# Attention and routed experts on one core: maxima 45 steps ahead, the router's product folded into the values', the last body's slots, scatters and pads interleaved anew

## The chip, the cores and the metric

The kernel runs on one core of a Trainium2 chip. The metric is the device time of one execution in microseconds (us), as the median of several runs. Lower is better.

## What is computed

Sixteen sequences of 750 frames with 23 features go through three layers. What matters of the reference:

```python
# 1. five neighbouring frames (115 values) -> 128, relu, batch norm: h is (16, 746, 128)
y = relu(einsum('blf,of->blo', patches, W) + b)
h = (y - mean) * rsqrt(var + eps) * gamma + beta
# 2. attention, 8 heads of 16
xn = layernorm(h)
q, k, v = split_heads(xn @ Wq.T + bq), ...
h = h + merge(softmax(q @ k.T * scale) @ v) @ Wo.T + bo
# 3. one of 8 experts per token
x = layernorm(h)
logits = x @ Wr + br
e, gate = top_1(logits), softmax(top_1)        # gate of one logit
h = h + gate * (relu(x @ W1[e] + b1[e]) @ W2[e] + b2[e])
```

## The kernel before

Every engine has its own program, written out by hand, and the programs meet in semaphores only. After the first layer (PE, ScalarE and VectorE pass all 16 sequences once) the work is a software pipeline of **bodies**, numbered -2 to 16. Body `i` has 72 **steps** on PE, ScalarE and VectorE. In body `i` the scores of sequence `i` are made, the maxima of sequence `i+1` (and the rest of `i`), the projections of sequence `i+2`, and the output, second layer norm and router of sequence `i-1`.

A step on PE is a scores product (written to a bank of three, which ScalarE exponentiates, lines 863 and 866), a maxima product (to another bank of three, which VectorE reduces, lines 1179 and 1182), and at some steps a product of the probabilities with the values (`weigh`, line 1366). Steps 0 to 23 and 36 to 59 are wide (512 columns), the others narrow (2 x 234). Steps 0 to 35 are heads 0 to 3, steps 36 to 71 heads 4 to 7. The maxima run `LEAD` steps ahead of the scores, with

```python
def maximum_of(i, s):
    return (i, s + LEAD) if s + LEAD < STEPS else (i + 1, s + LEAD - STEPS)
```

The scores subtract the maximum of their row through two more rows of the queries. These rows take a path of their own: VectorE finishes the maxima of a half (`maxima`, lines 979, 984 and 990), PE transposes them (tasks `MAX0` and `MAX1`, line 1321), ScalarE copies them (line 794), SyncE writes them into the queries by two DMAs (lines 552 and 541), and PE waits for these before step 0 (`MAX0`, heads 0 to 3 of the next body) or step 36 (`MAX1`) in `pe.wait_ge(s_mrow, ...)`.

The other products are **tasks**: `HTOK` (h transposed to rows of tokens, and in the same bank its product with the router's weights `wr_c`), `PROJ` (attention's output, with the router's columns beside it), `XNT`, `Q`, `K`, `V`, `RANK`. All share one PSUM bank in the loop, so each waits until the one before it was emptied. The order is written down in tables of step numbers: `FILLS` (when PE does a task), `EMPTY_AT` (when ScalarE empties it), `LN1_AT`, `LN2_AT`, `REST_AT`, `T_AT`, `ROUTE_AT`, `RANK_AT` (VectorE).

The router's logits of `h + attention` are put together from the part of h (`h_wr`, 8 columns a token, from `HTOK`) and the part of attention (from `PROJ`). GpSimd (POOL) adds a constant row to `h_wr`, makes the norms, splits q and k, and issues the indirect DMAs that scatter finished rows to the experts' regions (`scatter`, line 650, six DMAs a sequence).

Last come the **slots**: 101 tiles of 128 rows, each loaded by SyncE (line 578), transposed (line 1386), multiplied by the weights of its expert (lines 1395 and 1407) with ScalarE between, finished on VectorE (`dve_turn`: line 1150, 1152, the copy of the weights for the slot three later, line 1141, and line 1157), and stored by an indirect DMA of POOL (`store_slot`, line 657). A slot's buffer is used again six slots later, and VectorE then waits for the store. The first 12 slots lie in body 16 between the last sequence's output, norm and routing, at the steps of `PE_SLOTS`, `ACT_SLOTS` and `DVE_SLOTS`:

```python
if is_body(i, LAST_BODY):
    store_slots(5, 9)
    scatter(i, i - 1)
    store_slots(9, 2 * ROUND)
```

Slots 0 to 71 take rows of the first 14 sequences alone (`early_table`, in body 15). For the rest VectorE makes a second table (`late_table`) after slots 17 and 23, and SyncE fills the end of each expert's region by eight DMAs of 130 KB (`pad_regions`, line 427), ahead of the load of slot 24.

Of the kernel before, what the change touches and what calls it, by code (L numbers as in the profile page):

```python
# [5 lines left out]
def audio_tower(  # L6
# [52 lines left out]
    assert SLOTS <= 128  # L59
    FAR = 1 << 20  # L60
# [15 lines left out]
    LEAD = 48  # L76
# [25 lines left out]
    with ctx:  # L102
# [3 lines left out]
        def sem(name):  # L106
# [11 lines left out]
                  for n in range(2)]  # L118
# [46 lines left out]
        wq_sb, wk_sb, wv_sb = (sb(n, [128, D]) for n in ("wq_sb", "wk_sb", "wv_sb"))  # L165
# [5 lines left out]
        wr_c = sb("wr_c", [128, E])  # L171
# [22 lines left out]
        pad_i = sb("pad_i", [1, E], i32)  # L194
# [89 lines left out]

        s_cw = sem("s_cw")
# [12 lines left out]
        FILLS = (("HTOK", 0, 6), ("HTOK", 1, 10), ("PROJ", 0, 12), ("PROJ", 1, 21), ("MAX1", 0, 27), ("XNT", 0, 35),  # L298
                 ("XNT", 1, 39), ("Q", 0, 41), ("Q", 1, 44), ("K", 0, 48), ("K", 1, 52), ("V", 0, 56),
                 ("RANK", 0, 58), ("MAX0", 0, 63), ("V", 1, 65))  # L300
        EMPTY_AT = {("HTOK", 0): 8, ("HTOK", 1): 10, ("MAX1", 0): 27, ("XNT", 0): 36, ("XNT", 1): 39,
                    ("Q", 0): (41, 42), ("Q", 1): (44, 46), ("K", 0): (48, 49), ("K", 1): (53, 54), ("V", 0): 56,
                    ("MAX0", 0): 63, ("V", 1): 71}
# [118 lines left out]
        def pad_regions(engine, experts):  # L422

            engine.wait_ge(s_tab, 1)
            for e in experts:
                first = engine.value_load(pad_i[0:1, e:e + 1], min_val=0, max_val=DEAD - D)
                engine.dma_start(rows_dram[bass.ds(first, D), :], pad_row[:, :]).then_inc(s_pad, 16)
# [49 lines left out]
        def _(sp):  # L477
# [126 lines left out]
        def _(pool):  # L604
# [36 lines left out]
            def scatter(i, r):  # L641
# [880 lines left out]
```

## Time and profile before

| | |
|---|---|
| median of 3 runs | 1200.79 us (1198.47 to 1201.88) |
| the profiled execution | 1198.72 us, span 1197.0 us |
| PE busy | 1129.9 us, 94% |
| VectorE (DVE) busy | 1040.3 us, 87% |
| ScalarE (ACT) busy | 913.0 us, 76% |
| GpSimd (POOL) busy | 677.9 us, 57% |
| granted TensorE clock, mean | 0.971 |
| chain that ended last | PE 71%, DVE 16% |

All times of the trace are counted from the start of the span. A body of the loop takes some 55 us. Body 0 begins at about 101 us, body 16 at about 970 us. The busy time of overlapping matmuls is counted once; what a group of matmuls takes from PE is best read from the distance between the starts of two groups.

### The profile page before, as it was taken

Reading aid. Unit: us, or ns where it says so; the run is one execution under the profiler, and the core shown is the slowest. Engines: PE = TensorE matmul, PEld = TensorE weight load, DVE = VectorE, ACT = ScalarE, POOL = GpSimd, SP = SyncE. Lnnn points to the kernel's source line nnn. Section 1 sums busy time; section 2 is a strip of 40 time slices with the busy share of each in tenths; the row PEclk is TensorE's granted clock in tenths of the full one; section 3 lists DMA queues with packets and bytes.
Section 4 is the critical chain, followed back from the end, with each engine's and each line's share of the span. In section 5 each row is a group of like instructions: output and inputs, shape, how many; then the busy total and the mean of one; then the engine's idle time right before and its main releaser. Section 6 shows DMA issues by size and latency. Waiting matters only on the chain.

```text
span 1197.0 us, 52763 instructions
## 1 busy us (share of the span) xinstructions
PE 1129.9 (94%) x21251; PEld 743.9 (62%) x21251; DVE 1040.3 (87%) x2404; ACT 913.0 (76%) x2125; POOL 677.9 (57%) x894
## 2 busy tenths in 40 slices
PE   6579999999999999999999999999999988899996
PEld 3334656565656565565656565656565458799996
DVE  8569899999999999999999999999999746577774
ACT  5425888888888888888888888888887865477774
POOL 2052618575766657585847576565833446466664
PEclk9768999999999999999999999999999999899998
DMA  8052131423223231313132322313131613333331
GB/s 197 32 96 80 48 81 47 110 64 97 85 66 97 58 101 54 105 44 113 59 96 70 91 87 68 96 51 105 50 110 51 188 48 98 112 105 103 105 102 48
DMA packets 81200, 102.33 MB, mean 85 GB/s; under 512 B 17964, under 2 KB 74787, under 8 KB 80526
## 3 DMA queue, kind: packets, MB, share of 16 engines
q1 hardware_dynamic: 72416, 79.03, 24.8%
q0 software_dynamic: 8384, 20.22, 5.1%
q8 instruction: 159, 2.61, 1.0%
q14 instruction: 55, 0.45, 0.1%
q10 hardware_dynamic: 186, 0.02, 0.0%
HBM read 60.76 MB, written 38.93 MB: 83 GB/s over the span
## 4 chain that ended last, share of the span: by engine, by line
PE 71%; DVE 16%; issue 3%; DMA 2%; ACT 2%; SPq 1%; POOL 1%; DVEq 0%; POOLq 0%; ACTq 0%
PE psum L1301 39%; PE psum L1366 15%; DVE half_max L1179 7%; PE psum L1395 6%; PE psum L1407 6%; DVE half_max L1182 3%; PE psum L1306 2%; DVE stats L956 2%; DVE rows L1036 1%; ACT arena L863 1%; PE psum L1386 1%; DMA arena<-max_rows 1%; DVE merged_t L1017 1%; DMA routed_rows_dram<-rows,pos_i 1%; DVE seq L1141 0%
## 5 line engine op out<-in xcount | busy, mean ns | idle before, releaser
L1179 DVE TENSOR_REDUCE half_max<-psum 128x1 f32<-128x512 f32 x768 | 510.6, 678 | 36.0 <-PE psum L1301 32.8
L863 ACT ACTIVATE arena<-psum 128x512 f32<-128x512 f32 (+1 forms) x768 | 424.5, 602 | 62.8 <-PE psum L1301 53.7
L1301 PE MATMUL psum<-k_rows,arena 96*32 96x512 bf16 (+1 forms) x6144 | 463.7, 327 | 8.4 <-DMA k_rows<-k_parts_dram 4.4
L1301 PE MATMUL psum<-arena,k_rows 98*32 98x512 bf16 (+1 forms) x6144 | 457.9, 323 | 2.1 <-DMA arena<-max_rows 0.7
L1366 PE MATMUL psum<-arena,values 128*32 128x234 f32 (+3 forms) x3072 | 312.4, 476 | 1.0 <-ACT arena L866 0.8
L1301 PEld LDWEIGHTS psum<-k_rows,arena 96*32 96x32 bf16 x6144 | 180.0, 97 | 130.2 <-DVE half_max L1179 27.0
L1301 PEld LDWEIGHTS psum<-arena,k_rows 98*32 98x32 bf16 x6144 | 176.7, 96 | 132.7 <-issue 33.5
L1182 DVE TENSOR_REDUCE half_max<-psum 128x2 f32<-128x468 f32 x384 | 242.1, 630 | 2.8 <-PE psum L1301 2.7
L866 ACT ACTIVATE arena<-psum 128x468 f32<-128x468 f32 (+1 forms) x384 | 197.9, 570 | 32.3 <-PE psum L1301 30.7
L650 POOL DMA_INDIRECT routed_rows_dram<-rows,pos_i x96 | 97.0, 1011 | 92.2 <-PE psum L1301 51.3
L657 POOL DMA_INDIRECT out_dram<-k_rest,slot_id x85 | 98.6, 1160 | 68.1 <-DVE k_rest L1157 54.2
L1366 PEld LDWEIGHTS psum<-arena,values 128*32 128x32 f32 (+1 forms) x3072 | 96.2, 110 | 36.5 <-issue 4.2
L670 POOL TENSOR_TENSOR m_diff<-stats 128x6 f32<-128x6 f32 x15 | 3.0, 202 | 146.9 <-DVE stats L956 146.9
L844 ACT COPY xn_t<-psum 128x128 f32<-128x128 f32 x101 | 26.8, 265 | 74.3 <-PE psum L1386 71.3
L1395 PE MATMUL psum<-xn_t,values 128*128 128x128 f32 x536 | 71.8, 277 | 1.2 <-ACT xn_t L844 0.7
L407 POOL TENSOR_SCALAR rows<-rows,n_mean,rstd 128x128 f32<-128x128 f32 x90 | 72.4, 814 | 0.0
L407 POOL TENSOR_SCALAR arena<-h_cur,m_mean,rstd 128x128 f32<-128x128 f32 x90 | 70.5, 793 | 3.3 <-POOL rstd L696 3.2
L1395 PEld LDWEIGHTS psum<-xn_t,values 128*128 128x128 f32 x536 | 66.0, 194 | 2.2 <-issue 1.4
L1141 DVE COPY values<-seq 128x1156 f32 x67 | 52.7, 786 | 9.5
L416 POOL TENSOR_TENSOR q_rest<-q_full,q_part 128x746 f32<-128x746 f32 x15 | 24.2, 1615 | 46.8 <-DVE onehot L1066 29.8
L996 DVE STREAM_TRANSPOSE by_tok<-o_un 128x384 f32<-128x384 f32 x64 | 36.3, 567 | 14.7 <-ACT o_un L876 14.7
L1395 PE MATMUL psum<-xn_t,seq 128*128 128x128 f32 x272 | 38.4, 286 | 8.7 <-DVE seq L1141 8.2
(237 smaller groups left out, 1614.7 us busy)
## 6 DMA issues: line engine op xcount, KB each, us to landing
arena<-q_parts_dram SPq DMA_DIRECT2D x192, 93.2 KB, 2.5
k_rows<-k_parts_dram SPq DMA_DIRECT2D x192, 93.2 KB, 2.5
q_parts_dram<-q_part SPq DMA_DIRECT2D x48, 186.5 KB
k_parts_dram<-k_part SPq DMA_DIRECT2D x48, 186.5 KB, 1.9
q_full<-routed_rows_dram SPq DMA_DIRECT2D x34, 130.0 KB
k_full<-routed_rows_dram SPq DMA_DIRECT2D x34, 130.0 KB
q_rest<-routed_rows_dram SPq DMA_DIRECT2D x33, 130.0 KB
arena<-in_x_t_dram SPq DMA_DIRECT2D x3, 703.1 KB, 14.6
```

Source lines behind the costliest of these rows:

```text
L407: last = ops.tensor_scalar(dst(t), src(t), mean_var[:, t, 0:1], r_root[:, t:t + 1], ALU.subtract, ALU.mult)
L650: pool.indirect_dma_start(out=rows_dram, out_offset=bass.IndirectOffsetOnAxis(ap=pos_i[:, t:t + 1], axis=0), in_=rows[:, t, :], in_offset= ...
L657: pool.indirect_dma_start(out=out_rows, out_offset=bass.IndirectOffsetOnAxis(ap=slot_id[:, n:n + 1], axis=0), in_=slot_y[n][:, :], in_offs ...
L863: nc.scalar.activation(probs[0:kn(kt), kt % N_P, j, :], st_bank[s % N_ST][0:kn(kt), 0:WIDE_Q], ACT.Exp).then_inc(s_exp, 1)
L866: nc.scalar.activation(narrow_probs[0:kn(kt), kt, NARROW_Q * j:NARROW_Q * (j + 2)], st_bank[s % N_ST][0:kn(kt), 0:2 * NARROW_Q], ACT.Exp). ...
L1141: nc.vector.tensor_copy(slot_w[n % N_W].unsqueeze(1), w_sb[:, bass.ds(e, 1), :]).then_inc(s_fw, 1)
L1179: nc.vector.tensor_reduce(half_max[:, n, part:part + 1], mx_bank[m % N_MX][:, 0:WIDE_Q], AX.X, ALU.max)\
L1182: nc.vector.tensor_reduce(half_max[:, n, 2:4], mx_bank[m % N_MX][:, 0:2 * NARROW_Q].rearrange("p (a t) -> p a t", a=2), AX.X, ALU.max).the ...
L1301: last = nc.tensor.matmul(dst[n:n + m], weights[:, n:n + m], moving, start=start, stop=stop)
L1366: last = nc.tensor.matmul(o_bank[32 * j:32 * (j + 1), 0:WIDE_Q if wide else NARROW_Q], values[b % 3][0:kn(kt), kt, GH * g + j, :], moving, ...
L1395: last = nc.tensor.matmul(psum[:, 2 + n % 2, D * k:D * (k + 1)], slot_w[n % N_W][:, W1 + D * k:W1 + D * (k + 1)], slot_xt[n % 2][:, :], st ...
L1407: last = nc.tensor.matmul(psum[:, 5 + n % 2, 0:D], slot_ht[n % 2][:, D * k:D * (k + 1)], slot_w[n % N_W][:, W2 + D * k:W2 + D * (k + 1)], ...
```

## The change

- `LEAD` is 45 instead of 48, so all maxima stand three steps later against the scores, and `MAX0` and `MAX1` go from steps 63 and 27 to 66 and 30.
- The product of `h` with the router's weights leaves `HTOK`. The weights `wr_c` are now 8 more columns of `wv_sb`, so that `V` (128 columns before, 136 now) makes the product of the normed rows. ScalarE's copy to `h_wr` moves from `HTOK` to `V`. To undo the norm, POOL multiplies `h_wr` by the standard deviation (`std`), in two operations more a body, and `PROJ`'s reader waits for them (`s_hwr`).
- In body 16 POOL stores two slots after each scatter DMA, up to slot 23, instead of all six scatters in a row.
- One pad DMA stands ahead of each group of six loads from slot 24 to 71, instead of eight ahead of slot 24.
- The tables of steps are new.

```diff
-    LEAD = 48
+    LEAD = 45
+    PAD_FROM = EARLY // ROUND - E
-    LN1_AT = (13, 14, 17, 18, 20, 21)
-    LN2_AT = (30, 32, 33, 34, 35, 37)
+    LN1_AT = (11, 13, 15, 17, 18, 21)
+    LN2_AT = (29, 32, 33, 34, 35, 36)
...
-    DVE_SLOTS = {13: 0, 18: 1, 26: 2, 39: 3, 40: 4, 50: 5, 51: 6, 55: 7, 56: 8, 69: 9, 70: 10, 71: 11}
-    TABLE_AT, TABLE_T_AT, EARLY_AT, WEIGHTS_AT = 26, 30, 34, 44
+    DVE_SLOTS = {13: 0, 18: 1, 26: 2, 34: 3, 38: 4, 39: 5, 49: 6, 50: 7, 55: 8, 59: 9, 69: 10, 71: 11}
+    TABLE_AT, TABLE_T_AT, EARLY_AT, WEIGHTS_AT = 29, 39, 40, 45
...
# SyncE
-            with sp.Fori(2, 4) as v:
+            with sp.Fori(2, PAD_FROM) as v:
                 for u in range(ROUND):
                     load_slot(v * ROUND + u, u, v)
-            pad_regions(sp, range(E))
-            with sp.Fori(4, EARLY // ROUND) as v:
+            sp.wait_ge(s_tab, 1)
+            with sp.Fori(PAD_FROM, EARLY // ROUND) as v:
+                pad_region(sp, v)
                 for u in range(ROUND):
                     load_slot(v * ROUND + u, u, v)
...
# POOL, scatter
+                    if slots:
+                        last = 4 * ROUND if t == NT - 1 else 9 + slots * (t + 1)
+                        store_slots(9 + slots * t, last)
...
# POOL, body
-                    nc.gpsimd.tensor_tensor(h_wr[:, b % 4, :, :], h_wr[:, b % 4, :, :],
-                                            row_c[:, :].unsqueeze(1).to_broadcast([128, NT, E]), ALU.add)
+                    nc.gpsimd.tensor_tensor(std[:, b % 4, :], var_eps[:, :], rstd[:, :], ALU.mult)
...
+                    pool.wait_ge(s_free, fill(i - 1, "V", 1))
+                    nc.gpsimd.tensor_tensor(logits_of, logits_of, std[:, b % 4, :].unsqueeze(2).to_broadcast([128, NT, E]),
+                                            ALU.mult).then_inc(s_hwr, 1)
+                    pool.wait_ge(s_hwr, 2 * b + 1)
+                    nc.gpsimd.tensor_tensor(logits_of, logits_of, row_c[:, :].unsqueeze(1).to_broadcast([128, NT, E]), ALU.add)\
+                      .then_inc(s_hwr, 1)
...
# ScalarE
-                if name == "HTOK":
-                    nc.scalar.copy(h_wr[:, (i + 2) % 4, 3 * part:3 * (part + 1), :].rearrange("p t e -> p (t e)"),
-                                   bank(i, name, part)[:, 3 * D:3 * D + 3 * E])
...
+                both = bank(i, "V", k)[:, 0:3 * (D + E)].rearrange("p (t d) -> p t d", t=3)
+                nc.scalar.copy(h_wr[:, (i + 2) % 4, 3 * k:3 * (k + 1), :], both[:, :, D:D + E])
...
# PE
-                        last = quad(to[:, D * n:D * (n + 1)], xn_t[:, D * t:D * (t + 1)], wv_sb[:, :])
+                        last = quad(to[:, (D + E) * n:(D + E) * (n + 1)], xn_t[:, D * t:D * (t + 1)], wv_sb[:, :])
...
                     last = transposes(to, part, lambda t: h_t[:, D * t:D * (t + 1)])
-                    for n in range(3):
-                        t = 3 * part + n
-                        last = quad(to[:, 3 * D + E * n:3 * D + E * (n + 1)], h_t[:, D * t:D * (t + 1)], wr_c[:, :])
```

How the order moves, at three places. First PE in a body of the loop, from the transposes of `MAX0` to the end of the narrow steps. `arena,k_rows` with 234 columns is a narrow scores step, `k_rows,arena` the maxima, `arena,values` a `weigh`, `identb,max_parts` is `MAX0`, `wv_sb,xn_t` is `V`. Before:

```order
L1321 MATMUL psum<-identb,max_parts 24x128 x2
L1301 MATMUL psum<-arena,k_rows 32x234 x8
L1301 MATMUL psum<-k_rows,arena 32x512 x4
L1301 MATMUL psum<-arena,k_rows 32x234 x8
L1301 MATMUL psum<-k_rows,arena 32x234 x8
L1301 MATMUL psum<-wv_sb,xn_t 32x128 x12
L1301 MATMUL psum<-arena,k_rows 32x234 x8
L1301 MATMUL psum<-k_rows,arena 32x512 x4
L1301 MATMUL psum<-arena,k_rows 32x234 x8
L1301 MATMUL psum<-k_rows,arena 32x512 x4
L1366 MATMUL psum<-arena,values 32x234 x4
```

After, from the same task on:

```order
L1334 MATMUL psum<-identb,max_parts 24x128 x2
L1314 MATMUL psum<-arena,k_rows 32x234 x8
L1314 MATMUL psum<-k_rows,arena 32x512 x4
L1376 MATMUL psum<-arena,values 32x234 x4
L1314 MATMUL psum<-arena,k_rows 32x234 x8
L1314 MATMUL psum<-k_rows,arena 32x234 x8
L1376 MATMUL psum<-arena,values 32x234 x4
L1314 MATMUL psum<-arena,k_rows 32x234 x8
L1314 MATMUL psum<-k_rows,arena 32x512 x4
L1314 MATMUL psum<-wv_sb,xn_t 32x136 x12
```

Three steps less stand between `MAX0` and step 0 of the next body, and the second part of `V` stands later and has 136 columns.

Second, VectorE in body 16, from the end of slot 2 to slot 4: the statistics of the last layer norm (`BN_STATS`, `BN_AGGR`) and slot 3 (`k_rest` from `k_full`, with the copy of weights into `seq`). Before:

```order
L1157 SCALAR_TENSOR_TENSOR k_rest<-k_rest,k_full 128x128
L956 BN_STATS stats<-rows 128x6 x6
L964 BN_AGGR mv<-stats 128x2 x6
L967 TENSOR_SCALAR var_eps<-mv 128x6
L1137 TENSOR_LOAD xn_t
L1137 ISA x2
L1150 COPY slot_id<-k_full 128x1
L1152 TENSOR_TENSOR k_rest<-psum,seq 128x128
L1141 ISA
L1141 COPY seq<-seq 128x1156
```

After:

```order
L968 BN_STATS stats<-rows 128x6 x4
L1150 TENSOR_LOAD xn_t
L1150 ISA x2
L1163 COPY slot_id<-k_full 128x1
L1165 TENSOR_TENSOR k_rest<-psum,seq 128x128
L1154 ISA
L1154 COPY seq<-seq 128x1156
L1170 SCALAR_TENSOR_TENSOR k_rest<-k_rest,k_full 128x128
L968 BN_STATS stats<-rows 128x6 x2
L976 BN_AGGR mv<-stats 128x2 x6
```

Slot 3 is now ahead of the last two statistics and of their aggregates. In the same way slots 5 and 7 moved ahead of the routing operations that they followed, and slot 9 stands behind `RANK`.

Third, POOL in body 16, from the first scatter of the last sequence. Before:

```order
L650 DMA routed_rows_dram<-rows,pos_i 97408x260 [waits s_gated,s_rk,s_ln2_p,s_ids]
L650 DMA routed_rows_dram<-rows,pos_i 97408x260 x5
L657 DMA out_dram<-k_rest,slot_id 11936x128 [waits s_fy] x2
L657 DMA out_dram<-xn_t,slot_id 11936x128 [waits s_fy]
L657 DMA out_dram<-k_rest,slot_id 11936x128 [waits s_fy] x5
```

After:

```order
L665 DMA routed_rows_dram<-rows,pos_i 97408x260 [waits s_gated,s_rk,s_ln2_p,s_ids]
L646 DMA out_dram<-k_rest,slot_id 11936x128 [waits s_fy] x2
L665 DMA routed_rows_dram<-rows,pos_i 97408x260
L646 DMA out_dram<-xn_t,slot_id 11936x128 [waits s_fy]
L646 DMA out_dram<-k_rest,slot_id 11936x128 [waits s_fy]
L665 DMA routed_rows_dram<-rows,pos_i 97408x260
```

The store of slot 9 stands behind one scatter DMA instead of six.

## Rows read from the trace of the kernel before

**Rows 1.** Windows: stretch, length, busy us (instructions) by engine, clock, DMA share, GB/s

```profile
241.80:297.00 55.20, 54.91 (x1221) 33.13 (x1224) 53.27 (x118) 47.06 (x99) 35.87 (x51) 1.00 0.28 80
...
975.00:1197.00 222.00, 199.67 (x1783) 196.95 (x1780) 152.12 (x453) 136.73 (x500) 126.43 (x113) 0.96 0.32 94
```

**Rows 2.** Groups by shape, PE: busy us, mean ns, idle before

```profile
L1301 PE MATMUL psum<-wv_sb,xn_t 128*32 128x128 f32 x768 | 27.7, 278 | 0.0
...
L1301 PE MATMUL psum<-wr_c,h_t 128*32 128x8 f32 x768 | 12.6, 183 | 0.0
```

**Rows 3.** Timeline, PE, `HTOK` in the loop: start us, us, what [idle before]

```profile
270.72 0.38 PE L1301 MATMUL psum<-wr_c,h_t 128*32 128x8 f32 x24
270.93 0.40 PE L1301 MATMUL psum<-arena,k_rows 98*32 98x512 bf16 x4
```

**Rows 4.** Timeline, PE: `MAX0`, steps 64, 65 and 0 (next body), `MAX1`, step 36

```profile
260.69 0.23 PE L1321 MATMUL psum<-identb,max_parts 128*24 128x128 bf16 x2
260.70 0.42 PE L1301 MATMUL psum<-arena,k_rows 98*32 98x234 bf16 x8
...
261.12 0.42 PE L1301 MATMUL psum<-arena,k_rows 98*32 98x234 bf16 x8
...
265.91 0.40 PE L1301 MATMUL psum<-arena,k_rows 98*32 98x512 bf16 x4
...
288.00 0.23 PE L1321 MATMUL psum<-identb,max_parts 128*24 128x128 bf16 x2 [0.22 <-DVE max_parts L990]
...
293.45 0.40 PE L1301 MATMUL psum<-arena,k_rows 98*32 98x512 bf16 x4
```

**Rows 5.** Timeline, VectorE, around `MAX0`

```profile
260.21 0.19 DVE L990 TENSOR_TENSOR max_parts<-neg_max,max_parts 128x24 bf16<-128x24 f32 x1
...
260.99 1.27 DVE L1179 TENSOR_REDUCE half_max<-psum 128x1 f32<-128x512 f32 x2
```

**Rows 6.** SyncE's row DMAs: timeline (`MAX0`, `MAX1`), then the chain at a late `MAX1`

```profile
261.53 1.54 SPq L552 DMA_DIRECT2D arena<-max_rows  x2
...
290.43 1.54 SPq L541 DMA_DIRECT2D arena<-max_rows  x2
...
621.36 0.75 SPq L541
...
622.15 3.51 DMA arena<-max_rows
```

**Rows 7.** Timeline, PE, first `HTOK` and body -1

```profile
39.89 0.51 PE L1301 MATMUL psum<-wr_c,h_t 128*32 128x8 f32 x24
40.33 0.90 PE L1306 MATMUL psum<-ident,h_t 128*128 128x128 f32 x3
...
95.44 0.28 PE L1321 MATMUL psum<-identb,max_parts 128*24 128x128 bf16 x2 [0.33 <-DVE max_parts L990]
...
100.57 0.64 PE L1301 MATMUL psum<-arena,k_rows 98*32 98x512 bf16 x4
```

**Rows 8.** Timeline, PE, idle and slow stretches of the slots

```profile
987.80 1.39 PE L1395 MATMUL psum<-xn_t,seq 128*128 128x128 f32 x8 [1.84 <-DVE seq L1141]
...
1003.70 1.16 PE L1395 MATMUL psum<-xn_t,seq 128*128 128x128 f32 x8 [1.39 <-DVE seq L1141]
...
1017.73 1.16 PE L1395 MATMUL psum<-xn_t,seq 128*128 128x128 f32 x8 [2.39 <-DVE seq L1141]
...
1025.88 1.87 PE L1395 MATMUL psum<-xn_t,seq 128*128 128x128 f32 x8 [2.19 <-DVE seq L1141]
...
1035.40 0.33 PE L1386 MATMUL psum<-ident,q_full 128*128 128x128 f32 x1 [2.95 <-DMA q_full<-routed_rows_dram]
```

**Rows 9.** Timelines, what held slots 15 and 24: VectorE, SyncE

```profile
1016.42 0.15 DVE L1150 COPY slot_id<-k_full 128x1 int32<-128x1 int32 x1 [3.38 <-DMA out_dram<-k_rest,slot_id]
...
1023.51 8.37 SPq L427 DMA_DIRECT2D routed_rows_dram<-pad_row  x8
```

**Rows 10.** Timeline, VectorE, body 15, while the experts' weights load

```profile
940.23 0.18 DVE L1034 TENSOR_TENSOR raw<-psum,h_wr 128x24 f32<-128x24 f32 x1 [0.64 <-DMA routed_rows_dram<-rows,pos_i]
```

More of the change, by code:

```diff
@@ L283, in audio_tower @@
         s_fy = sem("s_fy")
+        s_hwr = sem("s_hwr")
         s_cw = sem("s_cw")
@@ L295, in audio_tower @@
         FIRST_LOOP = 1
[L298 to L303, printed above, removed]
+        FILLS = (("HTOK", 0, 6), ("HTOK", 1, 10), ("PROJ", 0, 12), ("PROJ", 1, 21), ("MAX1", 0, 30), ("XNT", 0, 35),
+                 ("XNT", 1, 39), ("Q", 0, 41), ("Q", 1, 44), ("K", 0, 47), ("K", 1, 52), ("V", 0, 56),
+                 ("RANK", 0, 58), ("MAX0", 0, 66), ("V", 1, 69))
+        EMPTY_AT = {("HTOK", 0): 7, ("HTOK", 1): 11, ("MAX1", 0): 30, ("XNT", 0): 36, ("XNT", 1): 39,
+                    ("Q", 0): (41, 42), ("Q", 1): (44, 45), ("K", 0): (48, 49), ("K", 1): (52, 54), ("V", 0): 56,
+                    ("MAX0", 0): 66, ("V", 1): 71}
         STAGE = {"V": 2, "MAX1": 0, "HTOK": 2, "XNT": 2, "PROJ": -1, "Q": 2, "MAX0": 1, "K": 2, "RANK": -1}
@@ L357, in run_bodies, with run_slots @@
                 body(i, i % 2)
-        def run_slots(engine, ahead, turn, behind=None):
-            for s in range(2 * ROUND, 4 * ROUND):
+        def run_slots(engine, ahead, turn, behind=None, first=2 * ROUND):
+            for s in range(first, 4 * ROUND):
                 turn(s, s % ROUND, s // ROUND)
@@ L420, in split, with pad_region @@
             ops.tensor_tensor(part[:, 2, :], rest[:, :], part[:, 1, :], ALU.subtract).then_inc(s_split, 1)
[L422 to L427, printed above, removed]
+        def pad_region(engine, n):
+            first = engine.value_load(pad_i[0:1, bass.ds(n, 1)], min_val=0, max_val=DEAD - D)
+            engine.dma_start(rows_dram[bass.ds(first, D), :], pad_row[:, :]).then_inc(s_pad, 16)
         def wait(engine, semaphore, value):
@@ L639, in _, with store_slot, store_slots, scatter @@
             nc.gpsimd.tensor_tensor(bn_rstd[:, :], bn_var[:, :], minus_half[:, 0:1], ALU.pow).then_inc(s_bn_pow, 1)
-            def scatter(i, r):
+            def store_slot(s, n, r):
+                wait_apart(pool, s_fy, s + 1, s_apart_p)
+                pool.indirect_dma_start(
+                    out=out_rows,
+                    out_offset=bass.IndirectOffsetOnAxis(ap=slot_id[:, n:n + 1], axis=0),
+                    in_=slot_y[n][:, :], in_offset=None, bounds_check=NTOK - 1, oob_is_err=False)\
+                    .then_inc(s_out[n], 16)
+            def store_slots(first, last):
+                for s in range(first, last):
+                    store_slot(s, s % ROUND, s // ROUND)
+            def scatter(i, r, slots=0):
                 pool.wait_ge(s_ln2_p, ln2_p_done(r) + (MERGED + 4 if r < B - 1 else 4))
@@ L707, in body @@
                                             ALU.add).then_inc(s_ln_p, 1)
+                if live(i, 1):
+                    b = i + 1
+                    logits_of = h_wr[:, b % 4, :, :]
+                    pool.wait_ge(s_free, fill(i - 1, "V", 1))
[4 more added lines that the diff above has]
+                      .then_inc(s_hwr, 1)
                 if live(i, -1):
@@ L748, in body @@
                     store_slots(5, 9)
-                    scatter(i, i - 1)
-                    store_slots(9, 2 * ROUND)
+                    scatter(i, i - 1, 2)
             run_bodies(pool, body)
-            run_slots(pool, 0, store_slot)
+            run_slots(pool, 0, store_slot, first=4 * ROUND)
         @block.scalar
```

39 lines of the change are left out of this document (16 added, 23 removed).

## The prediction

> **What bounds the kernel now.** I read the windows by stage first. In a body of the loop PE is busy for 54.91 of 55.20 us at the full 2.4 GHz, VectorE for 53.27, ScalarE for 47.06 [rows 1]. So PE sets the pace, with VectorE 3% behind it: what PE sheds shortens a body only while VectorE can follow, and a wait put into PE's queue costs its full length. The last 222 us are the slots; there PE has 199.67 us of work at a mean clock of 0.96, and the other three engines less [rows 1]. Some 22 us of that stage are idle. I then read the timelines of PE for what stands just ahead of each idle stretch, and VectorE's, POOL's and SyncE's for why.
>
> **The loop, per body.** *HTOK.* One part's router product, 24 records, starts at 270.72 and the next group at 270.93: 0.21 us of PE's queue [rows 3]. Two parts are removed: -0.42 us. Bounds: nothing, if VectorE is the limit there, and 12.6 / 16 = 0.79 us by the busy time [rows 2]; the distance of starts is the measure of a queue, so I take 0.42. *V.* Its 48 records a body take 27.7 / 16 = 1.73 us [rows 2]; 8 columns more on 128 are at most 0.11, I take +0.10. *POOL and ScalarE.* The copies to `h_wr` are as many as before. POOL's two added operations lie in its 19 us of idle time a body [rows 1], and their reader comes two bodies later: nothing; without that cover they would cost some 0.6 us. Holding `V`'s bank for the added copy can delay `RANK` by 0.1 us at most, left in the range.
>
> *MAX0's wait.* Today the last maxima operation ends at 260.40 [rows 5] and PE transposes at 260.69 [rows 4]: 0.29 us of slack. Three narrow steps more now stand ahead of both. PE needs 0.42 us for one (260.70 to 261.12 [rows 4]), 1.26 in all; VectorE 0.63 (two reductions in 1.27 [rows 5]), 1.9 in all, and two of the ranks' small operations moved ahead of it. The slack turns into a wait of 0.3 to 0.8 us; VectorE has small gaps to give, so I take +0.40. *MAX1's wait.* PE already waits there for the same operation [rows 4]. The three steps add about 0.5 us of lag, but the first `LN1` statistic moves into an idle stretch of VectorE, the second output addition goes ahead, and the stalls that PE has behind `MAX1` are had in the wait instead. I take -0.10, between -0.3 and +0.3.
>
> *The row DMAs' deadline.* From `MAX0` to step 0 PE has 265.91 - 260.69 = 5.22 us; three steps fewer leave 3.96. The chain: transposes to SyncE's first issue is 0.84 us (260.69 to 261.53 [rows 4, 6]), and ScalarE must first do the exponentials that now lie ahead, some 0.35 more. With the transposes at 260.69 + 1.26 + 0.40 = 262.35 the issue is at 263.55 and step 0 is due at 266.31. At `MAX1` rows were there within 293.45 - 290.43 = 3.02 us of the first issue [rows 4, 6], which gives 266.57; at the late one it was 0.75 + 3.51 and some 0.04 between, 4.3 us [rows 6]. I take +0.10 a body as a mean; the late case is the second rival. What is queued behind the SyncE issues (stores of q and k, loads of the next heads) moves 2 us later, and those loads now have three steps more to arrive.
>
> Sum a body: -0.42 + 0.10 + 0.40 - 0.10 + 0.10 = +0.08, over 15 bodies **+1.2 us**. The loop should hardly move.
>
> **Its ends.** The first `HTOK` runs at 1.2 GHz and is on the path to the first scores: its router product takes 0.44 us there (39.89 to 40.33 [rows 7]), twice, **-0.9**. Body -1 makes three steps of maxima less before body 0, 1.9 us at VectorE's pace, but step 0 can't come sooner than `MAX0` plus 0.84 plus 2.5 to 3.0 us: 99.0 for 100.57 today [rows 7], **-1.5**. At the other end three steps of body 15 keep their maxima, 0.63 for some 0.55 us of ScalarE's: **+0.3**. In body 15 VectorE already waits 0.64 us for a scatter that shares the queues with the experts' weights [rows 10]; these loads now start two us later and the reader one step earlier: **+1.0** (0 to 2.2).
>
> **The slots.** (a) VectorE is held at slot 15 for the store of slot 9, which POOL issues behind six scatters: 3.38 us [rows 9], of which PE loses 2.39 [rows 8]. With one scatter ahead the store goes out some 6 us sooner: **-2.4**. The scatters end some 9 us later, and nothing needs them before slot 72, which is 90 us away. (b) The pads keep SyncE for 8.37 us [rows 9], and PE then waits 2.95 us for slot 24 [rows 8]. One pad in six loads is 1.05 us in 11: **-2.9**. (c) Behind that gap PE's clock falls to 1.2 GHz; a layer took 1.87 us for 1.16 behind the gap ahead of it [rows 8], and two layers of it are **-1.4**. (d) From 985 to 1004 PE is idle for 1.84, 0.5 and 1.39 us and slow for some 1.7 between [rows 8], 5.4 in all, since VectorE makes the norm's statistics and the ranks ahead of a slot's weights. Going through the new order with the same durations, slot 3's weights come 1.8 us sooner, the clock then holds, slot 4 waits 1 us instead, and layer one of slot 12 starts at 999.7 instead of 1003.7: **-4.0**. (e) The 2.19 us at 1025.88 [rows 8] are the second table's small operations; they stay, and are late next. Sum **-10.7 us**.
>
> **Total:** +1.2 - 0.9 - 1.5 + 0.3 + 1.0 - 10.7 = -10.6 us, on the profiled 1198.7 us that is 1188.1. The median of the runs is 2.1 us above this execution, so I forecast **1190 us**. A measurement can tell 0.3% from no change: 3.6 us, so faster is under 1197.2 and slower over 1204.4.
>
> **Where a rule of the skill and a row part.** The 24 router records took 0.21 us, 9 ns apiece, since four lie side by side in the array's columns [rows 3]. The Trainium skill, "TensorE: Matmul & The Clock Gate", section "Back-to-back issue gap", has a floor of about 25 ns from start to start however few the columns. By it the two parts would be 1.2 us a body and the forecast some 12 us lower, 1178; the row decides, and speaks against it.
>
> **Rivals.** *1. VectorE is the limit* (0.15). It has hardly a gap from step 57 to step 36 of the next body; if it also sets the pace at steps 6 to 12, PE's 0.42 us are given back as waits. For: 53.27 busy of 55.20. Against: it does wait for PE once between steps 11 and 12. Price 0.42 x 15 = 6.3: 1196.5.
>
> *2. The row DMAs come too late* (0.09). If they take the 4.3 us of the late case, step 0 waits until 263.55 + 4.3 = 267.85, 1.54 us instead of 0.1: 15 x 1.44 = 21.6, **1212, slower than before**. It decides from 0.7 us a body up, that is 3.6 us from issue to landing. For: 4.3 us is a row. Against: that was at `MAX1`, among twelve loads of keys and queries; at `MAX0` the queue holds little. The Trainium skill, "DMA: Bandwidth & Descriptors", section "Anatomy of one DMA — SWDGE (gpsimd) path", gives about 2.0 us of fixed time to any transfer. By it, from the second issue at 264.3, the rows land at 266.3 as PE wants them, the +0.10 goes, and the time is 1188.7; the 3.02 us agree, the late row doesn't.
>
> *3. The slots give a third only* (0.13): POOL's indirect stores (about 1.3 us each, two and a scatter in 3.9 us, two slots in 3.8) stay behind, or the table's gap grows by what went elsewhere. +7.1: 1197.
>
> *4. The loop gains* (0.13): VectorE is ahead at both maxima, no wait at `MAX0` and none at `MAX1`, 0.5 us a body less: 1182.5.
>
> The forecast itself has 0.46, from 1185 to 1195; 0.04 are left for other ways near no change. Faster: 0.46 + 0.13 + 0.11 of rival 1 + 0.05 of rival 3 = 0.75. Slower: rival 2, 0.09. Within 0.3%: 0.16. The range from 1180 to 1200 takes the forecast, rivals 1 and 3 and most of 4, and leaves 2 out.
>
> **What would show it.** A body of 55.1 to 55.4 us from window to window, `HTOK`'s transposes followed at once by scores, PE idle 0.3 to 0.6 us at `MAX0` with VectorE's line 990 as releaser, and next to nothing at step 0. Idle on `max_rows` DMAs above 0.7 us a body would be rival 2; a body still of 55.2 with VectorE's reductions as PE's releaser ahead of step 12, rival 1. In the slots: no wait of VectorE for `out_dram` near slot 15, no 2.9 us gap at slot 24, the table's gap unchanged. The forecast is wrong if a body is 0.4 us off, or if the slots' stage shortens by less than 6 us.

## The result: slower, 1209.4 us for 1200.3

The changed kernel takes **1209.41 us** (median, 1204.33 to 1213.71), the kernel before 1200.26 us (1198.21 to 1202.87) on the same chip: a ratio of 1.0079, with a 95% interval from 1.0060 to 1.0097. The forecast was 1190 us, with a range up to 1200. The profiled execution of the changed kernel takes 1213.48 us, with a span of 1211.0. That is at the upper end of its runs, so its trace shows somewhat more loss than a median run has.

### The profile after

Windows of the changed kernel: two bodies of the loop, and the slots' stage (columns as in [rows 1]).

```profile
298.10:354.40 56.30, 54.60 (x1172) 32.34 (x1176) 53.60 (x118) 47.23 (x99) 36.21 (x53) 1.00 0.29 78
354.40:412.20 57.80, 54.71 (x1173) 33.04 (x1176) 53.95 (x118) 47.25 (x99) 36.41 (x54) 1.00 0.27 76
997.00:1211.00 214.00, 198.32 (x1805) 195.06 (x1793) 154.08 (x455) 138.38 (x505) 127.77 (x114) 0.97 0.34 97
```

A body has less work for PE than before (54.60 busy for 54.91 [rows 1]) and takes longer: 1.7 and 3.1 us of it are idle, where 0.29 us were. The granted clock isn't the cause: it is 1.00 in both windows, and over the whole stretch from 130 to 850 us. From one `MAX0` to the next, over 12 bodies, the mean is (891.19 - 204.71) / 12 = 57.21 us; before it was 55.31. What PE waited for from 130 to 850 us, first before, then after (us in total, times, longest):

```profile
PE psum L1321 <- DVE max_parts L990: 2.9, 13, 0.2
PE psum L1301 <- DMA arena<-max_rows: 0.7, 2, 0.5
```

```profile
PE psum L1334 <- DVE max_parts L1002: 19.3, 25, 1.3
PE psum L1314 <- DMA arena<-max_rows: 8.7, 9, 1.5
```

Line 1002 is line 990 of before, `low = full - high`, the last operation of the maxima. Both waits are those the prediction spoke of, at `MAX0` and at step 0 (and their likes at `MAX1` and step 36), and both are larger than it said. The timeline of the changed kernel around `MAX0` shows the first:

```profile
317.62 0.25 DVE L996 TENSOR_REDUCE max_parts<-half_max 128x12 bf16<-128x24 f32 x2
318.00 1.50 POOL L424 TENSOR_TENSOR k_part<-k_rest,k_part 128x746 bf16<-128x746 f32 x1
318.46 1.08 DVE L1002 TENSOR_TENSOR max_parts<-neg_max,max_parts 128x24 bf16<-128x24 f32 x1
319.66 0.12 PEld L1334 LDWEIGHTS psum<-identb,max_parts 128*24 128x24 bf16 x2 [1.61 <-issue]
319.69 0.23 PE L1334 MATMUL psum<-identb,max_parts 128*24 128x128 bf16 x2 [1.26 <-DVE max_parts L1002]
319.95 0.52 ACT L804 COPY max_rows<-psum 24x128 bf16<-24x128 bf16 x2 [0.51 <-PE psum L1334]
320.50 2.01 SPq L554 DMA_DIRECT2D arena<-max_rows  x2
323.72 0.40 PE L1314 MATMUL psum<-arena,k_rows 98*32 98x512 bf16 x4
```

VectorE's operation on 24 columns takes **1.08 us**; it took 0.19 [rows 5]. It ends at 319.54, within 0.04 us of the end of POOL's subtraction of line 424 (318.00 + 1.50 = 319.50), the last step of the split of k. All 13 of the loop's `MAX0` (203.49 to 889.94) have 1.06 to 1.10 us, each begun 0.44 to 0.49 us after POOL's; those of the loop ahead of `MAX1`, where POOL does something else, have 0.17. The trace of before had one stretched case among 32, and the prediction didn't read it:

```profile
148.59 1.51 POOL L420 TENSOR_TENSOR k_part<-k_rest,k_part 128x746 bf16<-128x746 f32 x1
149.34 0.79 DVE L990 TENSOR_TENSOR max_parts<-neg_max,max_parts 128x24 bf16<-128x24 f32 x1
```

The second wait, at step 0, from the timeline of the changed kernel:

```profile
204.71 0.23 PE L1334 MATMUL psum<-identb,max_parts 128*24 128x128 bf16 x2 [1.25 <-DVE max_parts L1002]
205.53 1.54 SPq L554 DMA_DIRECT2D arena<-max_rows  x2
...
208.49 0.41 PE L1314 MATMUL psum<-k_rows,arena 96*32 96x234 bf16 x8
210.27 0.40 PE L1314 MATMUL psum<-arena,k_rows 98*32 98x512 bf16 x4 [1.37 <-DMA arena<-max_rows]
```

From the first issue to step 0 it is 210.27 - 205.53 = 4.74 us. Over all 32 places PE starts step 0 or 36 between 2.74 and 4.86 us after the first issue, and at 13 of them it waited, 11.2 us in all. Before, the same distance was about 4.4 us at `MAX0` and 3.7 at most `MAX1`, and most of the late transfers were hidden behind it. The traces hold them all the same, as updates of the rows' semaphore, which the views shown here don't print. The last update recorded for a pair of rows comes 2.7 to 2.9 us after the first issue at most places; it comes later than 3.0 us at 11 of 32 places before (the latest 4.30) and at 14 of 32 after (the latest 4.83). So the rows were about as late before. What changed is the time that stood in front of them.

The slots went as forecast. Timeline of PE in the changed kernel, its idle stretches there (to be held against [rows 8]); the last row but one is at the second table:

```profile
1012.82 1.16 PE L1405 MATMUL psum<-xn_t,values 128*128 128x128 f32 x8 [1.08 <-DVE values L1154]
...
1017.71 1.16 PE L1405 MATMUL psum<-xn_t,seq 128*128 128x128 f32 x8 [0.82 <-DVE seq L1154]
...
1044.53 1.24 PE L1405 MATMUL psum<-xn_t,seq 128*128 128x128 f32 x8 [2.10 <-DVE seq L1154]
...
1045.79 1.91 PE L1417 MATMUL psum<-values,h_t 128*128 128x128 f32 x8
```

No wait is left at slots 15 and 24. The distance from the last `MAX1` to the transposes of `slot_cols`, well into the slots, is a measure that the loop hardly touches: 1040.00 - 945.03 = 94.97 us before, 1053.85 - 969.29 = 84.56 after, 10.4 us less. (`MAX1` itself stands three steps later now; counted from step 36 of body 15, which didn't move, it is 90.00 and 79.92 us, 10.1 less.) The start went as forecast too (body 0 begins at 98.46 for 100.57 [rows 7]), and `HTOK`: its transposes are at 328.05, the next scores at 328.52.

So some 12 us were won at the two ends, and the loop lost some 26: at the last `MAX1` the kernel is 24.3 us behind, though it started body 0 2.1 us ahead.

### The profile page after: what moved, and what is told of

Read it like the earlier page. It is cut to its first block, busy times and chain, and to the rows that moved or that the text cites. A ratio compares the mean times of both kernels' runs of the same rounds, so it can differ in the third digit from the quotient of the medians.

```text
span 1211.0 us, 51282 instructions
## 1 busy us (share of the span) xinstructions
PE 1118.9 (92%) x20483; PEld 730.8 (60%) x20483; DVE 1050.5 (87%) x2404; ACT 915.9 (76%) x2125; POOL 685.2 (57%) x926
## 4 chain that ended last, share of the span: by engine, by line
PE 59%; DVE 24%; DMA 5%; ACT 3%; issue 2%; SPq 1%; DVEq 0%; POOL 0%; POOLq 0%; ACTq 0%
PE psum L1314 32%; PE psum L1376 12%; DVE half_max L1192 11%; PE psum L1405 7%; PE psum L1417 6%; DVE half_max L1195 5%; DMA arena<-max_rows 4%; PE psum L1319 2%; DVE max_parts L1002 1%; ACT arena L878 1%; PE psum L1396 1%; DVE stats L968 1%; ACT arena L875 1%; DVE by_tok L1008 1%; DVE rows L1049 1%
## 5 line engine op out<-in xcount | busy, mean ns | idle before, releaser
L1314 PE MATMUL psum<-k_rows,arena 96*32 96x512 bf16 (+1 forms) x6144 | 457.4, 325 | 11.4 <-DMA k_rows<-k_parts_dram 5.8
L1314 PE MATMUL psum<-arena,k_rows 98*32 98x512 bf16 (+1 forms) x6144 | 453.5, 322 | 13.3 <-DMA arena<-max_rows 11.2
L1314 PEld LDWEIGHTS psum<-arena,k_rows 98*32 98x32 bf16 x6144 | 174.1, 96 | 158.7 <-issue 40.4
L1314 PEld LDWEIGHTS psum<-k_rows,arena 96*32 96x32 bf16 x6144 | 173.5, 97 | 136.9 <-DVE half_max L1192 22.9
L878 ACT ACTIVATE arena<-psum 128x468 f32<-128x468 f32 (+1 forms) x384 | 203.1, 566 | 61.2 <-PE psum L1314 59.7
L420 POOL TENSOR_TENSOR q_rest<-q_full,q_part 128x746 f32<-128x746 f32 x15 | 24.3, 1617 | 60.0 <-DVE onehot L1079 44.8
```

The lines of the kernel that those rows point to most:

```text
L878: nc.scalar.activation(narrow_probs[0:kn(kt), kt, NARROW_Q * j:NARROW_Q * (j + 2)], st_bank[s % N_ST][0:kn(kt), 0:2 * NARROW_Q], ACT.Exp). ...
L1314: last = nc.tensor.matmul(dst[n:n + m], weights[:, n:n + m], moving, start=start, stop=stop)
```

## The experiments

Theory A: LEAD 45 puts `max_parts` under POOL's subtraction, which holds it up, and takes from the rows' DMAs the time they need now and then; the rest of the change is sound. The rivals: the fold of the router costs too (B); VectorE is late at `MAX0` anyway (C); what is won at `MAX0` is lost at step 0 (D).

### LEAD 48 in the changed kernel

```diff
-    LEAD = 45
+    LEAD = 48
...
-    RANK_AT = (57, 58, 59, 60, 63)
+    RANK_AT = (57, 58, 59, 62, 68)
...
-        FILLS = (("HTOK", 0, 6), ("HTOK", 1, 10), ("PROJ", 0, 12), ("PROJ", 1, 21), ("MAX1", 0, 30), ("XNT", 0, 35),
...
-                 ("RANK", 0, 58), ("MAX0", 0, 66), ("V", 1, 69))
+        FILLS = (("HTOK", 0, 6), ("HTOK", 1, 10), ("PROJ", 0, 12), ("PROJ", 1, 21), ("MAX1", 0, 27), ("XNT", 0, 35),
...
+                 ("RANK", 0, 58), ("MAX0", 0, 63), ("V", 1, 65))
```

(with the other tables of the loop as before.)

> The changed kernel with LEAD 48 and the loop's tables of steps of the kernel before; the folded router product and all that changed behind body 15 stay. Theory A (the 45 steps cost the loop some 28 us: a stretched VectorE operation and late rows of maxima, nothing else is wrong with the change): a body of 54.8 to 55.2 us, PE idle at both maxima together under 5 us in the run, and 1186 to 1190 us, the forecast of old for the rest of the change. Rival B (the fold costs as well: V's bank is held longer, POOL's two added operations push its splits): a body of over 55.5 us, 1194 us or more.

Measured: **1181.62 us**, ratio to before 0.9854 (0.9832 to 0.9876). A body is (862.96 - 203.47) / 12 = 54.96 us. PE's waits from 130 to 850 us, in this kernel:

```profile
PE psum L1334 <- DVE max_parts L1002: 2.9, 13, 0.2
PE psum L1314 <- DMA arena<-max_rows: 0.2, 1, 0.2
```

That is 27 us faster than the change as it is, and 1.5% faster than the kernel before. LEAD and its tables cost it all; rival B falls. It came out some 4 us below the expected range, half of it in the tail (below).

### The collision taken away, with LEAD 45

POOL makes the gate's two small operations ahead of k's last subtraction, so that this subtraction starts later:

```diff
+            if between:
+                between()
             engine.wait_ge(s_split, done + 2)
             ops.tensor_tensor(part[:, 2, :], rest[:, :], part[:, 1, :], ALU.subtract).then_inc(s_split, 1)
...
-                    split(pool, nc.gpsimd, s_apart_p, i, "K")
+                    split(pool, nc.gpsimd, s_apart_p, i, "K", gate if live(i, -1) else None)
```

> The changed kernel with one thing moved: POOL makes the gate's two small operations ahead of the last operation of k's split, not behind it, so that this split operation starts some 1.5 us later, when VectorE's max_parts operation is through. Theory A (VectorE's max_parts operation, 1.08 us for 0.17, is held by POOL's operation with two inputs from the same memory): max_parts takes 0.17 to 0.3 us everywhere, PE's wait at MAX0 falls from 1.25 to some 0.35 us, 13 bodies get 0.9 us back: 1196 to 1199 us. Rival C (VectorE is late at MAX0 anyway, and PE would wait for its reductions instead): no more than 3 us gained, 1206 us or more. Rival D (what is gained at MAX0 is lost at step 0, since the rows' DMAs are what ends last): the wait for max_rows rises by as much, 1205 us or more.

Measured: **1197.02 us**, 0.9985 (0.9967 to 1.0003), 11 to 12 us less than the change. Timeline of this kernel at `MAX0`:

```profile
318.78 1.36 POOL L755 TENSOR_TENSOR g_inv<-g_exp,minus_one 128x6 f32<-128x6 f32 x1
319.35 0.17 DVE L1008 TENSOR_TENSOR max_parts<-neg_max,max_parts 128x24 bf16<-128x24 f32 x1
...
319.67 0.23 PE L1340 MATMUL psum<-identb,max_parts 128*24 128x128 bf16 x2 [0.35 <-DVE max_parts L1008]
...
320.37 1.50 POOL L426 TENSOR_TENSOR k_part<-k_rest,k_part 128x746 bf16<-128x746 f32 x1
```

`max_parts` is back at 0.17 us, and PE's wait at 0.35, where 1.25 was. C and D fall: the wait didn't move to the reductions, and the waits for the rows are 10.7 us in the run for 11.2. A body is (880.32 - 207.26) / 12 = 56.09 us. What is left between this kernel and the one with LEAD 48 is 1.1 us a body.

A control, the same edit in the kernel with LEAD 48:

> A control for the run with the gate moved: the same move of POOL's two gate operations, but in the kernel with LEAD 48, where POOL's operation with two inputs does not meet max_parts. Theory A: nothing to win, 1180 to 1184 us like the kernel with LEAD 48 alone. If moving the gate is worth something by itself (its 12.4 us with LEAD 45 were not the collision): under 1178 us.

Measured: 1180.97 us, 0.9852 (0.9832 to 0.9872). The move is worth nothing where nothing collides.

### The collision put into the kernel before

First POOL's split operations in another order, in the kernel before:

```diff
-                    split(pool, nc.gpsimd, s_apart_p, i, "Q")
-                    split(pool, nc.gpsimd, s_apart_p, i, "K")
+                    split_both(pool, nc.gpsimd, s_apart_p, i)
...
+            for n, (name, full, rest, part) in enumerate(names):
+                engine.wait_ge(s_free, fill(i, name, 1))
+                ops.tensor_tensor(rest[:, :], full[:, :], part[:, 0, :], ALU.subtract).then_inc(s_split, 1)
+            for n, (name, full, rest, part) in enumerate(names):
+                wait_apart(engine, s_split, done + n + 1, counts)
+                ops.tensor_scalar(part[:, 1, :], rest[:, :], 1.0, None, ALU.mult).then_inc(s_split, 1)
+            for n, (name, full, rest, part) in enumerate(names):
+                engine.wait_ge(s_split, done + n + 3)
+                ops.tensor_tensor(part[:, 2, :], rest[:, :], part[:, 1, :], ALU.subtract).then_inc(s_split, 1)
```

> The kernel before with POOL's six split operations in another order (both rests, both high parts, both low parts), so that the low part of q, a POOL operation with two inputs, should run when VectorE makes max_parts ahead of MAX0. Theory A: where they overlap max_parts takes 0.5 to 1.3 us for 0.17 and ends when POOL's operation ends; PE has 0.29 us of slack there, so a body is some 0.3 to 0.6 us longer and the kernel is at 1204 to 1209 us. Rival C (the stretch is no property of the pair of operations, it comes with LEAD 45): max_parts stays at 0.17 us and the time at 1200 us.

Measured: 1199.0 us, 0.999 (0.9975 to 1.0005). It missed: the timeline of this kernel has

```profile
257.82 2.08 POOL L431 TENSOR_SCALAR k_part<-k_rest 128x746 bf16<-128x746 f32 x1
259.18 0.18 DVE L1003 TENSOR_TENSOR max_parts<-neg_max,max_parts 128x24 bf16<-128x24 f32 x1
...
259.88 1.50 POOL L434 TENSOR_TENSOR q_part<-q_rest,q_part 128x746 bf16<-128x746 f32 x1
```

The subtraction came 0.7 us too late. What it does show is that `max_parts` takes its 0.18 us when it begins 1.36 us into POOL's 2.08 us operation with one input (the first 0.7 us of such an operation are another matter, see the last section). So once more, with k's rest behind q's high part, by which POOL no longer waits for k in between:

```diff
+            order = (("Q", 0), ("Q", 1), ("K", 0), ("K", 1), ("Q", 2), ("K", 2))
```

(0 is the rest, 1 the high part, 2 the low part. SyncE's stores of the parts wait for the new positions.)

> The kernel before with POOL's split operations in the order q rest, q high, k rest, k high, q low, k low. By the timeline of the last try, where POOL reached this place 0.7 us too late to meet VectorE, q's low part (two inputs, 1.50 us) should now start some 0.3 us ahead of max_parts at MAX0. Theory A (two-input operations of POOL and VectorE exclude each other): max_parts takes 0.9 to 1.3 us for 0.17 and ends with POOL's operation; PE has 0.29 us of slack, so it waits 0.6 to 1.0 us at MAX0 in some 13 bodies: 1207 to 1212 us. Rival C (the stretch comes with LEAD 45, not with the pair): max_parts stays at 0.17 us, 1200 us.

Measured: **1211.14 us**, 1.0083 (1.0067 to 1.0099). Timeline of this kernel:

```profile
261.41 1.51 POOL L438 TENSOR_TENSOR q_part<-q_rest,q_part 128x746 bf16<-128x746 f32 x1
261.57 1.39 DVE L1007 TENSOR_TENSOR max_parts<-neg_max,max_parts 128x24 bf16<-128x24 f32 x1
...
263.10 0.23 PE L1338 MATMUL psum<-identb,max_parts 128*24 128x128 bf16 x2 [0.88 <-DVE max_parts L1007]
```

The same six operations in another order on an engine that is 57% busy cost the kernel before 10 us. VectorE's operation starts 0.16 us after POOL's and ends 0.04 us after its end; a body is 56.00 us for 55.31. The body shown is the worst: in the other 12 of the loop `max_parts` starts 0.46 to 0.49 us after POOL's operation and takes 1.05 to 1.09 us, and PE waits 0.54 to 0.57 us. The 13 waits are 7.4 us together; the rest of the 10 us wasn't looked into. The collision belongs to the pair, not to LEAD 45.

### LEAD 45 with the old tables

Only `MAX1`, `MAX0` and `V`'s second part stand at their new steps:

```diff
-    ROUTE_AT = (42, 43, 44, 45, 49, 51)
-    RANK_AT = (57, 58, 59, 60, 63)
+    ROUTE_AT = (42, 43, 44, 45, 48, 51)
+    RANK_AT = (57, 58, 59, 62, 68)
```

(and so the other tables of the loop.)

> The changed kernel with LEAD 45, MAX1, MAX0 and V's second part at their new steps, but the other tables of the loop (statistics, transposes, routing, ranks, emptying) as before. Theory A (LEAD alone costs the 28 us, the other tables can't repair it): 1206 to 1214 us, with max_parts stretched at MAX0. If the new tables were needed to hold LEAD 45: 1215 us or more. If it is the new tables that hurt: under 1200 us.

Measured: 1205.14 us, 1.0041 (1.0025 to 1.0057). `max_parts` in this kernel (ns, shortest, median, longest):

```profile
L1002 DVE TENSOR_TENSOR max_parts<-neg_max,max_parts x32: 172/176/853, 94.1 to 964.7; 128x24 bf16<-128x24 f32 x32
```

It collides here as well, for 0.82 to 0.85 us: POOL began its subtraction 0.69 to 0.73 us ahead of it, not 0.46. The new tables repair nothing; they cost another 0.4%, which the two intervals only just tell apart. Some 3 us of it are the longer overlap (13 x 0.25); the rest wasn't looked into.

### The rows' second DMA on a queue of its own

```diff
# SyncE: the first row only; ScalarE, behind its own copy:
+                act.wait_ge(s_free, fill(i, name, 0))
+                act.dma_start(q_rows[par][KR + 1:KR + 2, GH * g:GH * (g + 1), :],
+                              max_rows[g][QUAD:QUAD + GH * NT, :]).then_inc(s_mrow, 16)
```

> The kernel of the run with the gate ahead of k's low part (1197.0 us), with the second of the two rows of maxima issued by ScalarE behind its own copy, while SyncE issues the first; both queues issue at once. Theory E (behind the stretched operation it is the rows' late landing at steps 0 and 36 that is left of the loop's loss; the second issue, 0.77 us after the first, sets it): the waits for max_rows fall from 10.7 us to under 4 us in the run, 1188 to 1193 us. Rival F (the landing is late because of the other transfers on the DMA engines, not because of the second issue): the waits stay above 8 us, 1196 us. Rival G (ScalarE is held by its issue and its exponentials come late): waits of PE for ScalarE's exponentials rise, 1198 us or more.

Measured: 1194.91 us, 0.9956 (0.9943 to 0.9969). PE's waits from 130 to 850 us in this kernel, then in the one that it was made from (the gate moved):

```profile
PE psum L1339 <- DVE max_parts L1007: 8.7, 26, 0.4
PE psum L1319 <- ACT arena L883: 3.0, 12, 0.5
PE psum L1319 <- DMA arena<-max_rows: 0.7, 2, 0.3
```

```profile
PE psum L1320 <- DMA arena<-max_rows: 8.6, 9, 2.0
PE psum L1340 <- DVE max_parts L1008: 8.3, 25, 0.3
```

The waits for the rows are gone, 8.6 us down to 0.7. By the updates of the semaphore the rows are there 2.1 to 2.4 us after the first issue at most places, for 2.7, and later than 3.0 us at 3 of 32, for 11. So the two transfers on one queue come later, and late more often. That the second transfer was the late one each time isn't shown, since both update one semaphore. But the time fell by 2 to 3.5 us only, and a body from 56.09 to 55.92: PE now waits for ScalarE's exponentials (line 883), which stand behind ScalarE's own wait and issue. Both E and G held in part.

### The tail in pieces

Each in the kernel before, whose LEAD, tables of the loop and router stay.

```diff
# pads_only
-            pad_regions(sp, range(E))
+                pad_region(sp, v)
# inter_only
-                    scatter(i, i - 1)
-                    store_slots(9, 2 * ROUND)
+                    scatter(i, i - 1, 2)
# pads_inter: both; tail_only: both and the tables (PE_SLOTS, ACT_SLOTS and the steps of the first table too)
-        DVE_SLOTS = {13: 0, 18: 1, 26: 2, 39: 3, 40: 4, 50: 5, 51: 6, 55: 7, 56: 8, 69: 9, 70: 10, 71: 11}
+        DVE_SLOTS = {13: 0, 18: 1, 26: 2, 34: 3, 38: 4, 39: 5, 49: 6, 50: 7, 55: 8, 59: 9, 69: 10, 71: 11}
```

> The kernel before with the pads spread, the scatters and stores interleaved and the new tables of the slots in body 16; LEAD, the loop's tables and the router's product as before. The prediction's slots' terms give -10.7 us: 1189 to 1191 us. If the tail gains only a third: 1196 us. The loop must read 55.2 us a body.

> The kernel before with the pads alone spread: one ahead of each group of six loads from slot 24. The terms (b) and (c) of the prediction together give -2.9 and up to -1.4 us: 1196 to 1197.5 us. If the loads of slots 24 and later are late anyway: 1200 us.

> The kernel before with POOL's stores and scatters of body 16 interleaved, two stores behind each scatter, and nothing else. The term (a) of the prediction gives -2.4 us: 1197.8 us. If the wait at slot 15 only moves to a later slot: 1200 us. What is left to the run of the whole tail, 12.9 us faster than before, goes to the slots' tables (the term (d), -4.0).

> The kernel before with the pads spread and the stores interleaved, without the new tables of slots. Alone the two gave 0.61% and 0.40%. If they add up, and the new tables bring next to nothing: 1187 to 1190 us, like the whole tail. If the tables bring the 4 us of the prediction's term (d): 1191 to 1194 us.

| | time, us | ratio (95%) | last `MAX1` to `slot_cols`, us |
|---|---|---|---|
| before | 1200 | 1 | 94.97 |
| pads alone | 1193.57 | 0.9939 (0.9925 to 0.9953) | 88.84 |
| interleaving alone | 1197.22 | 0.9960 (0.9943 to 0.9977) | 94.07 |
| both | 1189.78 | 0.9923 (0.9906 to 0.9940) | 84.99 |
| both and the tables | 1187.24 | 0.9900 (0.9882 to 0.9919) | 82.21 |

The whole tail gives 12 us, a little over the forecast. The last column is from one profiled execution each, and it isn't free of noise: in three kernels with the tail of before (before itself and the two with POOL's split reordered) it is 94.97, 95.73 and 97.14 us, and in the seven with the whole new tail 82.21 to 84.56. So only the pads' part is clear, 6.1 us by the column and 7.3 by the ratio. The interleaving is worth 0.9 us by the column and 4.8 by the ratio alone, 3.9 and 1.9 beside the spread pads; the tables are worth 2.8 by both, but their two intervals overlap. How these two share what is left isn't shown. The timeline of the kernel with the interleaving alone has the following:

```profile
1023.64 1.16 PE L1397 MATMUL psum<-xn_t,seq 128*128 128x128 f32 x8 [2.10 <-DVE seq L1143]
...
1034.02 0.47 PE L1388 MATMUL psum<-ident,q_full 128*128 128x128 f32 x1 [5.43 <-DMA q_full<-routed_rows_dram]
```

PE comes to slot 24 sooner and waits 5.43 us there for the loads behind the pads, 2.95 in the kernel before [rows 8]. Its time is 4 to 5 us below that of before all the same, while its profiled execution shows only the 0.9; which of the two is right the runs don't settle. In that execution a collision fell ahead of body 0 too (`max_parts` at 94.70 took 1.49 us), and body 0 began 0.75 us later than in the kernel before.

## Why the prediction was wrong

**MAX0's wait: the step that failed, by a mechanism it didn't have.** It said +0.40 us, from three narrow steps of VectorE's against the slack. Without the collision that is what is measured, 0.35 at `MAX0`. In the changed kernel it is 1.25, since the operation itself grew by 0.91 us. The prediction moved `max_parts` three steps along VectorE's queue and took its duration from where it had stood; it didn't look at what POOL does there. It spoke of POOL for the two added operations only, and put them at nothing since POOL had idle time. Yet [rows 4, 5] gave the place, and the timeline of POOL before gave the neighbour:

```profile
261.73 1.51 POOL L420 TENSOR_TENSOR k_part<-k_rest,k_part 128x746 bf16<-128x746 f32 x1
```

By the prediction's own 1.9 us, `max_parts` was to go from 260.21 to some 262.1, into this subtraction. This one term cost 11 to 12 us. The slack of 0.29 us was misread besides: PE starts its transposes 0.15 us after the end of `max_parts` where it does wait for it (319.54 to 319.69), so only 0.14 us of it were to spare. None of the rivals named the collision; rival 2 came nearest in its total (1212), but its mechanism gave half of its price, so that its total came near by luck.

**The row DMAs' deadline: mis-sized.** +0.10 us a body was taken, with the late case as rival 2. Measured are 11.2 us of waits in the run, 0.7 a body, the very point from which rival 2 was said to decide. The prediction took the 3.02 us of one `MAX1` for the rule and 4.3 for the exception. With a distance of 4.4 us ahead of most steps 0, a transfer that took 4 us left no wait and no row in the views that it read. The semaphore's updates in the trace of before had them: 11 of 32 were later than 3.0 us. An estimate from these 11, with the distance of about 3.0 us that three steps less leave, is 8.2 us of waits in the run, 0.55 a body, for the 0.10 taken. What the prediction holds against rival 2, that the late row was at `MAX1` where the queue is full, doesn't stand either: the longest waits of the changed kernel (1.37, 1.4, 1.5 and 1.49 us) are at both places. The section of the Trainium skill that it names there is on transfers that GpSimd issues, while these are SyncE's. As a price the waits don't add up cleanly, as the run with two queues shows.

**MAX1's wait:** -0.10 was taken, 0.34 for 0.22 is measured, +0.12; inside its bounds.

**HTOK and V: right.** -0.42 + 0.10 = -0.32 us a body; the kernel with LEAD 48 differs from that with the tail alone by the fold: a body of 54.96 us for 55.29, and 1181.62 us for 1187.24, -5.6 where -4.8 and -0.9 were forecast. So the row was rightly preferred to the floor of about 25 ns from start to start in the Trainium skill ("TensorE: Matmul & The Clock Gate", "Back-to-back issue gap"), by which the fold would have given 1.1 us a body, as an estimate; 0.33 are measured.

**The ends: right where they were looked at.** Body 0 starts 2.1 us earlier for 2.4 forecast. In body 15 VectorE waits 1.47 us for the scatter where it waited 0.64 [rows 10], 0.8 more for 1.0 forecast. The 0.3 of body 15's maxima wasn't measured by itself. The wait for the rows at body 15 (1.16 us at step 36) is in the waits above.

**The slots: right in the sum** (-10.7 forecast; -10.4 by one execution of the changed kernel, -12 by the runs of the kernel with the tail alone), not clearly in the parts: the pads were worth 6.1 to 7.3 and not 4.3. For the interleaving (2.4 forecast) and the tables (4.0 forecast) the runs give no split that stands clear of the noise.

The sum with the measured loop: (57.21 - 55.31) x 15 = 28.5, less 2.1 and 10.4, is +16; the profiled executions differ by 14.8, the medians by 9.2. The spread of the changed kernel is wide (1204.3 to 1213.7), and the profiled one is at its upper end. Of the 1.90 us a body the waits explain 1.25 at `MAX0`, 0.12 at `MAX1` and some 0.6 at steps 0 and 36, less the 0.33 that the fold gives; about 0.3 stay unexplained.

## What to carry to other kernels

When an instruction moves, its duration moves with it only if what the other engines do at its new place is the same: read the neighbours there, POOL's beside VectorE's above all, and look at the longest of a group's durations (0.79 us beside a median of 0.17), not only its mean. And a transfer's latency that was never waited for leaves no row among the waits; whoever cuts the time that stands in front of it must count the landings themselves (the semaphore's updates, if the trace has them), or take that time as the bound, not the shortest latency seen. Here the best kernel is the change without its first part: the router folded, the tail interleaved, LEAD left at 48, 1181.6 us.

## What the hardware showed that was not expected

- A subtraction of VectorE with both inputs in SBUF (0.17 us alone) that starts while POOL runs a `TENSOR_TENSOR` over 746 columns ends with it: 1.06 to 1.10, 0.82 to 0.85 and up to 1.39 us in three kernels, each time within about 0.05 us of POOL's end. Where the two start within 0.01 us of each other, as at 95.12 in the kernel before, VectorE's takes its 0.17 and POOL's 1.55 instead of 1.51. The Trainium skill, "SBUF — State Buffer", section "Who interferes with whom", has this: a VectorE instruction with two SBUF inputs contends with a GpSimd instruction that reads SBUF, over a pair of ports that is an exclusive lock, and the order of issue decides who blocks. The traces agree for this pair of operations.
- POOL's `TENSOR_SCALAR` over 746 columns (2.11 us, one input) holds VectorE only at its start. In the kernel before:

```profile
254.10 2.11 POOL L418 TENSOR_SCALAR q_part<-q_rest 128x746 bf16<-128x746 f32 x1 [0.51 <-POOL q_rest L416]
254.32 1.00 DVE L1008 TENSOR_TENSOR arena<-by_tok,r_den 128x384 f32<-128x384 f32 x1
```

  This product of VectorE takes 0.54 us alone. Begun 0.22, 0.41 or 0.54 us after POOL's operation it takes 1.00, 0.81 or 0.68 us and ends 1.22 us after POOL's start each time, as if it could begin at 0.67 us and not before. `max_parts` was never begun earlier than 0.63 us into such an operation, so its 0.17 to 0.21 us there don't show that an operation with one input is harmless. So the hold lasts here for the first third of POOL's operation and not for the whole; why isn't shown.
- POOL's power of 6 columns, 1.36 us long, doesn't hold `max_parts` (0.17 us) that begins 0.56 us or more after its start. VectorE's reductions, which read PSUM, are at 0.68 and 0.63 us whatever POOL does.
- Two small DMAs issued some 0.8 us apart on one queue let PE go on 2.74 to 4.96 us after the first issue. At the latest places (before, changed, gate moved) all recorded updates of their semaphore but one had come by some 2.7 us, and the last came at 4.2 to 4.9. With each DMA on a queue of its own PE waited twice, for 0.7 us in all, at distances of 2.4 to 3.6 us.
- PE's wait of 1.99 us at step 0 (at 154.20 in the kernel with the gate moved) was followed by scores at half the pace, 0.66 us for 0.40 a group, their starts 0.43 us apart for 0.22, until some 3.5 us later. The granted clock was 0.50 there (1.2 GHz, from 156.0 to 157.7) and 1.00 (2.4 GHz) from 157.7 on. None of the waits of up to 1.5 us in the loop of the changed kernel did this. So a late row can cost more than its wait.
